# First attention without a query copy, key searches deferred past the scalings, attention set-up reordered, and a last mixture computed by groups of batches

## What is computed

```
layer 0: q = LN(x) W^T + b ; s = q . ctx^T + (1 - mask) * NEG ; x += softmax(s) ctx     (one head)
         y = LN(x); four times: y = max prob * (silu(y w1[e]) w2[e]), e = best of 16 experts, 512 wide
         x += y
layers 1-3: 16 heads of 8 columns; k and v of the layer from the context (layer 2 masked, layer 3
         with normalised q and k); x += softmax(q k^T / sqrt(8)) v wo + bo
         layer 1: gated part of one expert; layer 2: the 8 best of 64 experts, 32 wide, and 2 shared
layer 3: gates = softmax(LN(x) Wg), 8 experts 512 wide, the best 2 per row, weights w1, w2 of sum 1,
         a row counts at an expert while its place in the order of arrival is below C = 2*K*T/e
         x += sum over the 2 of w * kept * (gelu(LN(x) W1[e] + b1[e]) W2[e] + b2[e])
```

## Time and profile before

| | before |
|---|---|
| median of 3 runs | 2509.19 us (2508.78 to 2511.66) |
| profiled execution: time, span | 2497.96 us, 2496.2 us |
| mean granted TensorE clock | 0.916 |
| busy: PE, DVE, ACT, POOL | 85%, 52%, 58%, 10% of the span |
| instructions | 44542 |

### The profile page before, as it was taken

One profiled execution on the slowest core, in us unless ns is written; L12 is line 12 of the kernel. 1 busy time (PEld: TensorE's weight loads), 2 busy tenths in 40 slices (PEclk: granted clock), 3 DMA queues, 4 the chain that ended last, 5 costly groups with the idle time before them and its releaser, 6 DMA issues. The chain is left out here.

```text
span 2496.2 us, 44542 instructions
## 1 busy us (share of the span) xinstructions
PE 2116.4 (85%) x17610; PEld 1451.4 (58%) x17610; DVE 1296.2 (52%) x1701; ACT 1457.8 (58%) x1766; POOL 239.8 (10%) x307
## 2 busy tenths in 40 slices
PE   4766988979889469999846999988956999976998
PEld 2543755847658246666534666655644666655886
DVE  4553443334333466666467777754456666643111
ACT  2334446445554558888735888875435888862333
POOL 1005023141330400000010000010010000000000
PEclk9996999979989779999968999998978999986999
DMA  5758446355463548788235777831036778710000
GB/s 173 226 178 282 169 157 227 113 190 196 159 232 112 169 111 186 187 186 187 66 83 123 186 186 186 186 79 35 0 81 145 185 187 186 186 47 1 26 17 22
DMA packets 119703, 352.73 MB, mean 141 GB/s; under 512 B 20122, under 2 KB 54800, under 8 KB 118896
## 3 DMA queue, kind: packets, MB, share of 16 engines
q1 hardware_dynamic: 105568, 321.35, 47.4%
q0 software_dynamic: 13936, 28.59, 4.0%
HBM read 257.58 MB, written 91.23 MB: 140 GB/s over the span
## 5 line engine op out<-in xcount | busy, mean ns | idle before, releaser
L947 ACT ACTIVATE a_probs<-a_score 128x1200 f32<-128x1200 f32 x768 | 858.0, 1169 | 203.4 <-PE a_score L860 203.4
L860 PE MATMUL a_score<-a_qstack,a_kstack 128*128 128x400 f32 x2304 | 552.2, 372 | 56.9 <-DVE a_qstack L1030 56.0
L860 PEld LDWEIGHTS a_score<-a_qstack,a_kstack 128*128 128x128 f32 x2304 | 379.9, 190 | 226.9 <-issue 177.1
L822 PE MATMUL a_numer<-a_probs,a_v 128*18 128x200 f32 (+1 forms) x9216 | 470.9, 335 | 0.0
L822 PEld LDWEIGHTS a_numer<-a_probs,a_v 128*18 128x18 f32 (+1 forms) x9216 | 228.2, 97 | 184.2 <-issue 88.1
L1021 DVE TENSOR_TENSOR a_kstack<-a_kraw,a_kstack 64x2888 fp32r<-64x2888 f32 x90 | 284.8, 3164 | 2.8
L1030 DVE TENSOR_TENSOR a_qstack<-a_qrep,k_groupmask 128x1600 fp32r<-128x1600 f32 x48 | 87.6, 1825 | 173.5 <-PE a_score L860 144.4
L1016 DVE CAST a_kstack<-a_kraw 128x2888 fp32r<-128x2888 f32 x90 | 149.8, 1665 | 10.7 <-DVE a_own L1081 9.3
L1572 ACT ACTIVATE f3d_hidden<-f3d_ph,f_b 128x400 f32<-128x400 f32 x128 | 76.1, 594 | 116.5 <-PE f3d_ph L1530 109.2
L1782 PEld LDWEIGHTS f0r_ph<-f0r_xsT,f0r_w 128*128 128x128 f32 x896 | 119.3, 198 | 30.0 <-issue 12.0
L1782 PE MATMUL f0r_ph<-f0r_xsT,f0r_w 128*128 128x128 f32 x896 | 123.1, 282 | 8.9 <-DVE f0r_xsT L1963 8.9
(11 more groups left out here) (370 smaller groups left out, 2754.2 us busy)
## 6 DMA issues: line engine op xcount, KB each, us to landing
a_kraw<-keys SPq DMA_DIRECT2D x384, 361.0 KB, 7.2
values<-kv_vst SPq DMA_DIRECT2D x32, 1296.0 KB, 5.5
a_v<-values SPq DMA_DIRECT2D x48, 864.0 KB, 5.8
keys<-kv_made SPq DMA_DIRECT2D x48, 722.0 KB, 5.3
l0a_ctxT<-in_ctxT SPq DMA_DIRECT2D x16, 722.0 KB, 6.4
kv_ctxT<-in_ctxT SPq DMA_DIRECT2D x16, 722.0 KB, 8.2
l0a_ctx<-in_ctx SPq DMA_DIRECT2D x16, 704.0 KB
l0a_mask<-in_mask_BxSxS_ik SPq DMA_DIRECT2D x16, 564.1 KB
```

The source lines that it names most:

```text
L822: last = pe.matmul(numer[32 * g:32 * g + PC, p * 2 * SQ:(p + 1) * 2 * SQ], v[0:rows(t), j, t, (2 * g + p) * PC:(2 * g + p + 1) * PC], prob ...
L860: last = pe.matmul(to, kstack[:, j, g * SK + t * 128:g * SK + (t + 1) * 128], qstack[:, j, g * GH:(g + 1) * GH, :], start=True, stop=not s ...
L947: act.activation(probs[:, n % NP, :].rearrange("p (g q) -> p g q", g=SPAN), slot_ps[:, n % 2, :, 0:GQ], ACT.Exp, scale=HSCALE).then_inc(ex ...
```

## The change

Four parts. First attention: no `q1`; the copy to `probsT` in three pieces of 4, 4 and 3 blocks, each waited for on its own; the scores loop written out. Rounds: `keys_dve` split into `normals_dve` and `largest_dve`, and another order on VectorE; a round's last two searches run in the next round, or at the end of the last. Attentions: `wo2`'s 16 transfers move into the main block; low keys, blocked queries and masked values of batch 0 stand between flag and branch. Last mixture: one scope, group by group with all eight experts' weights held; it also stores each group of the output, and `all_experts`, `Experts` and `write_out` are gone.

```diff
             def scores(b, h, j):
                 pe.wait_ge(ctxT_in[j], 16 * h + 16)
-                pe.wait_ge(q1_ready, b + 1)
-                pe.wait_ge(kept, b + 1)
+                pe.wait_ge(kept, 4 * b + 4)
                 for at, n in KCHUNKS:
-                    last = pe.matmul(ps[0:SQ, j, at:at + n], q1[:, j, :], ctxT[:, j, at:at + n],
+                    last = pe.matmul(ps[0:SQ, j, at:at + n], qT[:, b, :], ctxT[:, j, at:at + n],
...
-                last.then_inc(turned, 1)
-                pe.wait_ge(kept, b + 3)
+                    if t % 4 == 3:
+                        last.then_inc(turned, 1)
                 pe.wait_ge(ctx_in[j], 32 * h + 32)
                 pe.wait_ge(added, b + 1)
                 for t in range(KT):
+                    if t in (0, 4, 8, KT - 1):
+                        pe.wait_ge(kept, 4 * b + (9, 10, 11, 12)[(0, 4, 8, KT - 1).index(t)])
...
             def turns(b, j):
-                act.wait_ge(turned, b + 3)
                 act.wait_ge(outed, b + 1)
-                act.copy(probsT[:, j, 0:KT - 1, :],
-                         ps[:, j, 0:128 * (KT - 1)].rearrange("p (t q) -> p t q", q=128)[:, :, 0:SQ]).then_inc(step, 1)
+                for r in range(3):
+                    act.wait_ge(turned, 3 * b + 7 + r)
+                    n = 4 if r < 2 else 3
+                    act.copy(probsT[:, j, 4 * r:4 * r + n, :],
+                             ps[:, j, 512 * r:512 * r + 128 * n].rearrange("p (t q) -> p t q", q=128)[:, :, 0:SQ]).then_inc(kept, 1)
...
-                dve.tensor_copy(q1[:, j, :], qT[:, b, :]).then_inc(q1_ready, 1)
...
             pool.wait_ge(cleared, 3)
-            for h in range(H):
-                g, p, j = h // GH, h % GH // 2, h % 2
-                at = 32 * g + (HD + 1) * j
-                pool.dma_start(wo2[at:at + HD, p, :], ins[f"wo{layer}"][h * HD:(h + 1) * HD, :]).then_inc(wo_in, 16)
...
+        @block.gpsimd
+        def _(pool):
+            for h in range(H):
+                g, p, j = h // GH, h % GH // 2, h % 2
+                at = 32 * g + (HD + 1) * j
+                pool.dma_start(wo2[at:at + HD, p, :], ins[f"wo{layer}"][h * HD:(h + 1) * HD, :]).then_inc(wo_in, 16)
...
-            for half in range(2):
-                dve.wait_ge(k_high, half + 1)
-                low = kstack[64:128, 0, half * KHALF:(half + 1) * KHALF]
-                dve.tensor_tensor(low, kraw[64:128, half, :], low.bitcast(F32), ALU.subtract).then_inc(k_low, 1)
             dve.wait_ge(bound_full, 1)
...
-                block_queries(0)
-                if masked:
-                    mask_values(0)
...
+            for half in range(2):
+                low_keys(0, half)
+                if half == 0:
+                    block_queries(0)
+            if masked:
+                mask_values(0)
             dve.wait_ge(numer_free, 1)
...
+            if layer:
+                for n in (1, 2):
+                    maker.largest_dve(dve, mine[0] - 1, n)
             for b in early:
-                maker.keys_dve(dve, b, banks)
+                maker.normals_dve(dve, b, banks)
+                for n in (1, 2):
+                    maker.largest_dve(dve, b, n)
...
-            maker.keys_dve(dve, late[0], banks)
...
+            maker.normals_dve(dve, late[0], banks)
             scale(0)
-            maker.keys_dve(dve, late[1], banks, (lambda: scale(1), lambda: scale(2)))
+            for n in (1, 2):
+                maker.largest_dve(dve, late[0], n)
+            maker.normals_dve(dve, late[1], banks)
+            scale(1)
+            scale(2)
             if more:
                 pick(0)
-                pick(1)
-            scale(3)
-            if more:
-                pick(2)
-                pick(3)
+                scale(3)
+                for g in range(1, TG):
+                    pick(g)
+            else:
+                scale(3)
+                for n in (1, 2):
+                    maker.largest_dve(dve, late[1], n)
...
+            for e in range(E3):
+                sp.dma_start(w1[:, e, :], ins["L3_W1"][e]).then_inc(w_in[e], 16)
+                sp.dma_start(b1[:, e, :], ins["L3_b1"][e]).then_inc(w_in[e], 16)
+                sp.dma_start(w2[:, e, :, :], ins["L3_W2"][e].rearrange("(c p) d -> p c d", p=128)).then_inc(w_in[e], 16)
...
+            def down(n):
+                g, e = divmod(n, E3)
+                if e == 0 and g >= 2:
+                    pe.wait_ge(y_kept, g - 1)
+                pe.wait_ge(scaled, n + 1)
+                for ci in range(FC):
+                    pe.matmul(py[:, g % 2, 0:NTG], w2[:, e, ci, :], hidden[:, g % 2, e, ci, :],
+                              start=(e == 0 and ci == 0), stop=False)
...
+            pick(0)
+            pick(1)
+            for n in range(STEPS):
+                g, e = divmod(n, E3)
+                if n + E3 < STEPS:
+                    up(n + E3)
+                if n + 2 < STEPS:
+                    pick(n + 2)
+                down(n)
+                if e == 1 and g:
+                    back(g - 1)
+                if e == E3 - 1:
+                    pe.matmul(py[:, g % 2, 0:NTG], b2[:, :], own[:, g * NTG:(g + 1) * NTG].bitcast(F32),
+                              start=False, stop=True).then_inc(y_full, 1)
+            back(TG - 1)
```

More of the change, by code:

```diff
@@ L339, in outputs @@
                 last.then_inc(outed, 1)
+            pe.wait_ge(q_kept, TG)
             scores(0, 0, 0)
[L342 removed]
+            for i in range((B - 2) // 2):
                 scores(2 * i + 1, i, 1)
@@ L2139, in write_out, with l3_ffn, loads @@
-def write_out(nc, k, out):
-    with Scope(nc, "store") as c:
-        (stored,) = c.sems("stored")
+def l3_ffn(nc, k, ins, out):
+    with Scope(nc, "f3") as c:
+        wg = c.sb("wg", [128, E3])
+        b2 = c.sb("b2", [2 * E3, D])
+        w1 = c.sb("w1", [128, E3, FF])
+        w2 = c.sb("w2", [128, E3, FC, D])
+        b1 = c.sb("b1", [128, E3, FC])
+        r_in = c.sem("r_in")
+        w_in = c.sems(" ".join(f"w_in{e}" for e in range(E3)))
+        def loads(sp):
+            sp.dma_start(wg[:, :], ins["L3_Wg"]).then_inc(r_in, 16)
+            for part in range(2):
+                sp.dma_start(b2[part * E3:(part + 1) * E3, :], ins["L3_b2"]).then_inc(r_in, 16)
+            for e in range(E3):
+                sp.dma_start(w1[:, e, :], ins["L3_W1"][e]).then_inc(w_in[e], 16)
+                sp.dma_start(b1[:, e, :], ins["L3_b1"][e]).then_inc(w_in[e], 16)
+                sp.dma_start(w2[:, e, :, :], ins["L3_W2"][e].rearrange("(c p) d -> p c d", p=128)).then_inc(w_in[e], 16)
+        layernorm(nc, k, "ln3f", loads=loads)
+        logits, e_, probs, hit, rest = (c.sb(n, [SQ, B, E3]) for n in "logits e probs hit rest".split())
+        one, count, run, pos = (c.sb(n, [SQ, E3, 2, B]) for n in "one count run pos".split())
+        runs = c.sb("runs", [SQ, E3, 2 * B])
+        prod = c.sb("prod", [SQ, 2, B, E3])
+        pair = c.sb("pair", [SQ, 2, B])
+        top, total, inv, den = (c.sb(n, [SQ, B]) for n in "top total inv den".split())
+        gates = c.sb("gates", [SQ, B, E3])
+        weights = c.sb("weights", [SQ, B, 2, E3])
+        picker = c.sb("picker", [2 * E3, E3, 128], F32R)
+        own = c.sb("own", [2 * E3, NT], F32R)
+        hidden = c.sb("hidden", [128, 2, E3, FC, NTG])
+        yT = c.sb("yT", [128, 2, NTG])
+        ph = c.ps("ph", [128, 3, 512])
+        pw = c.ps("pw", [128, 2, 512])
+        py = c.ps("py", [128, 2, 512])
+        pt = c.ps("pt", [128, 512])
+        routed, exp_ready, exped, ones_ready, counted, weighted, turned, own_ready, picker_made = c.sems(
+            "routed exp_ready exped ones_ready counted weighted turned own_ready picker_made")
+        up_full, gelued, w_full, scaled, y_full, y_kept, back_full, added, step, stored = c.sems(
+            "up_full gelued w_full scaled y_full y_kept back_full added step stored")
+        turn_ps = (py[:, 0, :], py[:, 1, :], pt[:, :], pw[:, 0, :])
+        STEPS = TG * E3
+        TURN, COUNT = 5, 2
```

376 lines of the change are left out of this document (149 added, 227 removed).

## The result

The changed kernel takes 2413.74 us (median of 4 runs, 2411.59 to 2415.51) where the kernel before took 2508.99 (4 runs beside it). The ratio is 0.962, 95% interval 0.9603 to 0.9636: 95 us faster, 21 us short of the forecast, and 0.7 us outside its range. The profiled execution has a span of 2411.1 us and a mean clock of 0.927.

A forecast was written before the change was run, and what follows sets the result against it. TensorE was taken as the bound, nearly full in steady stretches, with avoidable work or idle gaps elsewhere. Terms 25.0 + 12.1 + 9.5 + 22.1 + 47.9 = 116.6 us off the 2509.19 median gave 2392.6 us, range 2374 to 2413.

The forecast's parts named there:

- first attention: First attention: removing one TensorE pause and shortening another cuts the cycle from 9.0 to 7.2 us, gaining 25.0 us.
- rounds: Mixture rounds: VectorE's searches deferred and scalings moved ahead gain 14.6 us, less 2.5 in the last round: 12.1 us.
- barrier: Ahead of attentions 1 to 3: moving GpSimd's 16 small transfers opens the all-engine barrier sooner, gaining 9.5 us.
- branch: Ahead of attentions 1 to 3's batches: VectorE work moved before the branch lets TensorE start earlier, gaining 22.1 us.
- last mixture: Last mixture: grouped 400-column down products, steps of 5.56 us, and up products not waiting for routing gain 47.9 us.
- two transfer bounds: First attention: DMA transfers fill 6.6 us per cycle and the mask request loop takes 6.7, both under 7.2.
- Rival (a): First attention: transfers bound it, the cycle stays 8.6 us, the gain is 5, time 2412.6 us; chance 0.17.
- rival (d): Last mixture's loop: TensorE's clock drops to the lower level, making the kernel slower, up to 2582 us; chance 0.02.
- the pick is 0.18: Last mixture: the added pick product costs 0.18 us a step, derived from a layer-2 step, giving steps of 5.56 us.
- its 1.2: Mixture rounds' end: the first scaling, placed ahead of the searches, starts 1.2 us earlier, limited by its gather.
- The cost in the last round: Last mixture round: with no next round to cover the deferred searches, they cost 2.5 us (1.6 to 3.2).
- 2.8 come back: Attentions' batch 1: with the branch pause unchanged, its keys end at 918.2, due 915.5, giving back 2.8 us.

The follow-up runs named there:

- with two masks: The changed kernel loading only the masks of batches 0 and 1 in the first attention and using them for all later batches: 2380.15 us, 0.9544 of the kernel before.
- the second profile: The changed kernel itself, nothing altered, run and profiled again as a reference: 2399.43 us against 2495.14 for the kernel before, ratio 0.9619.

## Why the prediction was wrong

By its own terms, in us: first attention 25.0 forecast, 10 to 12 by the stages and 7 alone; rounds 12.1, 8 to 10; barrier 9.5, 10 by the times and 14.7 by the stages; branch 22.1, 24 to 29; last mixture 47.9, 38 to 39. Two terms were too large by 24 together, and the two terms of the attentions, 31.6 together, too small by 6 to 8 (38 alone, 39.5 by the stages). It is because these errors partly cancel that the time lies only 0.7 us outside the range.

- **First attention: the step that failed.** The prediction wrote of the two transfer bounds, "Both are under 7.2, so TensorE stays the bound, narrowly". What TensorE loses by itself was right: both pauses went, and with two masks the cycle is 7.1. But 6.6 us of DMA time per cycle in the earlier trace rows was taken as a floor that a cycle of 7.2 could come within 0.6 us of. It would need a share of 0.92, from a queue in which each request waits for a buffer. The runs held 0.86 in the changed kernel and 0.94 at best. Nor is the transfers' price fixed: a kilobyte took 52.8 ns in the kernel before and 56.1 in the changed one, 52.5 to 63.3 in its variants, so the cycle's 6.6 us became 7.1 (0.86 of 8.3). Rival (a) named this, with a cycle of 8.6; it was 8.3. Some 7 of the missing 13 us are then TensorE's clock, 0.50 behind four of the waits, a cost that the prediction put at nothing for this stage: rival (d) weighed it for the last mixture only. That is worked out from the rows; no run has these waits without the slower clock.
- **Last mixture: a term mis-sized.** The mechanism was right (400-column products, step without the routing). "So the pick is 0.18" came from a product with 128 rows of weights; here the weights have 16, and the row gives 0.57. Padded to 128 rows the step is the forecast 5.56, and the stage 11.9 us shorter (all 32 steps have a pick, not only the 24 full ones). That is more than the 9.5 us by which the term missed: the rest of the stage came out 2.4 us shorter than the prediction worked it through.
- **Rounds: right, a little high.** In the second profile the way from the first scaling to the first pick is 3.1, 4.5 and 3.1 us shorter in rounds 0 to 2 (3.3 forecast), and from there to the next round 0.7, 1.6 and 0.7 (0.35 forecast). The first scaling gave nothing of its 1.2: it stands 0.8 and 0.4 us later and 0.2 earlier, since its gather lands no sooner. The cost in the last round was 3.2 for 2.5, and could be avoided.
- **Barrier: right in mechanism, and in size or a little low.** The small transfers held it, and the second key half is what was late next. Alone the part gave 10 us, with 14.7 by the stages.
- **Branch: right in mechanism, the pause wrongly placed.** The prediction put the 9.5 us behind the remainders and took the middle of two ends. (Its lower end of 17.3 does not follow from its own "2.8 come back", which gives 18.5; the middle would be 22.7.) As it seems, the sequencer takes the branch while the engine still works off its queue, and the fetch meets few key loads then. Neither the pause nor the wait at batch 1 came.
- **The reference.** The forecast took terms from a profile 11 us faster than the median it was set against. That did no harm here: the ratio is 0.9619 where ScalarE's pauses are absent and 0.962 where they are present.

## What to carry to other kernels

When a wait is removed from a pipelined loop, compare the new cycle with the transfer time per cycle at a share that a trace has shown to hold, not at 1.00. Here that was 0.73 before the change and 0.86 after it, and the forecast needed 0.92. Look at the granted clock of the stage too, since waits that move can bring it down. Take the cost of a small matmul from a row with the same number of weight rows, and read it from start to start. Work that must be done anyway belongs between the flag and the code behind the branch, and large loads behind both; both orders gained here, the second in one pair of runs only.

## What was not expected of the hardware

- A weight load of 16 rows did not run ahead beside 128-row matmuls here: 0.57 us for a product that costs 0.18 with 128 rows, zeros included. Whether 32 or 64 rows would do was not tried.
- A branch cost VectorE 3.7 us without and 9.5 us with key loads in flight, and nothing visible with 8 us of work ahead of the code behind it.
- 16 small transfers issued by GpSimd ahead of a barrier held it 8 to 9 us each time while large loads were in flight. It opened 2.4 to 2.6 us behind the last of their packets; whether a single such transfer would hold it as long was not tried.
- In the first attention of the changed kernel the granted clock fell to 0.50 for 3.4 us at a time (103.9 to 107.3 is one), in two profiles behind waits of 1.5 to 3.4 us and not behind every such wait, while the slower but regular cycle of the kernel before, with 2.3 us idle in each 9.0, kept it at 1.00.
- In some batches ScalarE stands still for 1 to 3 us at a time in the early keys of rounds 1 to 3, with nothing in the trace that ends the wait, and in these batches the kernel before is 11 us or more slower. It depends on neither the kernel nor the part changed, and it came on both chips. The cause stays open: instruction packets fall into almost none of these pauses.
